# A pre-norm block with routed experts on one core: expert runs in order of size, empty tiles last, four expert tiles between the last token steps

## What is computed

```python
# attn
qkv = einsum('btd,ed->bte', rms_norm(x), w_qkv); q, k, v = split(qkv, 3)
q, k = rms_norm(q), rms_norm(k)
w = exp(k); kv = w * v
y = sigmoid(q) * cumsum(kv, 1) / (cumsum(w, 1) + 1e-6)
u, g = split(einsum('bte,fe->btf', y, w_swiglu), 2)
return x + einsum('btd,ed->bte', u * silu(g), w_out)
# ffn: E = 8 experts, the best K = 2 of each token, summed without weights
logits = flat @ router_weight.T + router_bias
_, topk_idx = top_k(softmax(logits), 2)
y = einsum('th,ehk->tek', flat, weight) + bias[None]
out = take_along_axis(y, topk_idx[:, :, None], axis=1).sum(axis=1)
```

## Time and profile before

| | us |
|---|---|
| median of three runs | 1670.75 (1668.12 to 1671.56) |
| the profiled execution | 1668.43 |
| its span, first to last instruction | 1666.6 |
| TensorE busy | 1589.8 (95%) |
| VectorE busy | 1206.2 (72%) |
| GpSimd busy | 975.3 (59%) |
| ScalarE busy | 568.0 (34%) |
| mean granted TensorE clock | 0.984 of full speed |

### The profile page before, as it was taken

One profiled execution on the slowest core, in us unless ns is written; L12 is line 12 of the kernel. 1 busy time (PEld: TensorE's weight loads), 2 busy tenths in 40 slices (PEclk: granted clock), 3 DMA queues, 4 the chain that ended last, 5 costly groups with the idle time before them and its releaser, 6 DMA issues. The chain is left out here.

```text
span 1666.6 us, 27354 instructions
## 1 busy us (share of the span) xinstructions
PE 1589.8 (95%) x7986; PEld 1298.2 (78%) x7986; DVE 1206.2 (72%) x2434; ACT 568.0 (34%) x1088; POOL 975.3 (59%) x1257
## 2 busy tenths in 40 slices
PE   7999999999999999999999999989999778999987
PEld 4788888788878887887888788778888556888866
DVE  6777778777876787788777767887887465666654
ACT  4333333333333333333333333323332232444432
POOL 4445566575567566755765575557553374666652
PEclk9999999999999999999999999999999897999999
DMA  7022333334333333333333333333424599279996
GB/s 249 29 91 89 115 126 131 119 114 165 115 114 115 115 140 114 137 129 135 133 122 115 115 140 114 115 140 115 140 93 163 151 344 339 84 258 353 383 376 243
DMA packets 138938, 265.64 MB, mean 159 GB/s; under 512 B 18615, under 2 KB 19393, under 8 KB 138794
## 3 DMA queue, kind: packets, MB, share of 16 engines
q1 hardware_dynamic: 121994, 229.70, 39.6%
q0 software_dynamic: 16800, 34.21, 5.9%
HBM read 316.28 MB, written 101.11 MB: 250 GB/s over the span
## 5 line engine op out<-in xcount | busy, mean ns | idle before, releaser
L741 DVE RECIPROCAL B<-B 128x512 f32<-128x512 f32 x64 | 214.6, 3353 | 2.2
L361 POOL TENSOR_SCALAR sa<-ss,hinv,ep 128x1 f32<-128x1 f32 x128 | 44.3, 346 | 211.9 <-ACT B L547 211.2
L446 POOL DMA_INDIRECT out_dram<-B,tab x91 | 94.3, 1036 | 108.9 <-DVE B L817 82.3
L375 POOL TENSOR_TENSOR F<-B,F 128x512 fp32r<-128x512 f32 x64 | 82.4, 1288 | 122.8 <-ACT F L569 122.8
L401 POOL TENSOR_TENSOR B<-B 128x512 f32<-128x512 f32 x112 | 143.3, 1300 | 0.0
L406 POOL TENSOR_TENSOR R<-B,R 128x512 fp32r<-128x512 f32 x112 | 142.0, 1288 | 0.0
L355 POOL TENSOR_SCALAR B<-B,nm,r 128x512 f32<-128x512 f32 x64 | 49.2, 769 | 109.4 <-DVE B L769 109.0
L1238 PE MATMUL pK<-R,F 128*128 128x512 f32 x256 | 108.0, 422 | 1.9 <-DVE B L715 1.9
L1238 PE MATMUL pG<-R,F 128*128 128x512 f32 x256 | 106.8, 417 | 1.9 <-POOL F L375 1.9
L1238 PE MATMUL pU<-R,F 128*128 128x512 f32 x256 | 106.4, 416 | 0.0
L1238 PE MATMUL pV<-R,F 128*128 128x512 f32 x256 | 100.8, 394 | 2.2 <-DVE B L715 2.2
(11 more groups left out here) (237 smaller groups left out, 4606.7 us busy)
## 6 DMA issues: line engine op xcount, KB each, us to landing
R<-pair_weights SPq DMA_DIRECT2D x91, 2048.0 KB
pair_weights<-R SPq DMA_DIRECT2D x112, 512.0 KB, 3.9
B<-in_wm SPq DMA_DIRECT2D x112, 256.0 KB, 3.1
B<-pair_biases SPq DMA_DIRECT2D x91, 256.0 KB
x_scratch<-B SPq DMA_DIRECT2D x64, 264.0 KB, 2.1
B<-in_x SPq DMA_DIRECT2D x64, 256.0 KB, 3.7
B<-in_xt SPq DMA_DIRECT2D x32, 256.0 KB, 3.9
XTB<-in_xt SPq DMA_DIRECT2D x32, 256.0 KB
```

Source lines behind the costliest of these rows:

```text
L361: p.tensor_scalar(sa[:, r, j:j + 1], ss[:, r, j:j + 1], hinv[:, 0:1], ep[:, r:r + 1], ALU.mult, ALU.add).then_inc(s[f"ra{j}"], 1)
L375: p.tensor_tensor(fr(3)[0], DD, fr(2)[1], ALU.subtract).then_inc(s["yl"], 1)
L446: p.indirect_dma_start(od, bass.IndirectOffsetOnAxis(ap=idx[:, J:J + 1], axis=0), YO[J % 3], None, bounds_check=T * 128 - 1, oob_is_err=Fa ...
L741: v.reciprocal(DD, DD).then_inc(s["rec"], 1)
```

## The change

1. `table(0)` orders the early pairs by number of whole tiles, ties by index: a key per pair, a 28x28 comparison, two reductions and a product in place of a running sum. `table(1)` computes each pair's end the same way from the run order.
2. The left-over late runs go to the last pairs of the order and no longer to the first.
3. TensorE's order at the end has four expert runs (0 to 3) between the last token steps, and all engines' orders follow: gathers 0 to 6 are issued in steps 60 to 63, `xn(0)` and `xn(1)` in step 62, `load_pair(3)` ahead of the store of tile Z-1, scatters 0 and 1 ahead of tile Z's normalisation. Runs 1 and 3 keep their transposed parts in slot 2 of R (`HL`), so `load_pair(4)` waits until run 3 is done. `XN[1]` moves to another block of B.
4. In ranks steps two `side` operations at most stand ahead of the gate besides the regular ones, and `side(6)` follows `hc`. In the expert runs `side(9)` takes the place of `side(7)`; the last block's routing starts at J = 6, with RM_J, TT_J, IT_J = 8, 12, 16.

```diff
-        XN = [blk(26), TH_]
+        XN = [blk(26), blk(27)]
...
+        def HL(J):
+
+            if J in (1, 3):
+                at = 2 * 4096 + J // 2 * 1024
+                return R[:, at:at + 512], R[:, at + 512:at + 1024]
+            return fr(2 * (J % 2))[0], fr(2 * (J % 2) + 1)[0]
...
-        RM_J, TT_J, IT_J = 5, 11, 14
+        RM_J, TT_J, IT_J = 8, 12, 16
...
@@ load_pair
+                if t == 4:
+                    e.wait_ge(s["MM"], 4)
...
@@ sync_program
             load_pair(2)
+            load_pair(3)
             store(Z - 1)
-            for t in range(3, 7):
+            for t in range(4, 7):
                 load_pair(t)
...
@@ pool_program
-                if i == Z - 1:
-                    gather(0)
-                    gather(1)
-            for J in range(2, 5):
-                gather(J)
+                if i >= Z - 3:
+                    for J in range(2 * (i - Z + 3), min(2 * (i - Z + 3) + 2, 7)):
+                        gather(J)
             yl(Z)
             x2n(Z - 1)
+            scatter(0)
+            scatter(1)
             x2n(Z)
...
-            asked_ids, asked = False, 5
-            for J in range(1, NJ):
+            asked_ids, asked = False, 7
+            for J in range(3, NJ):
...
@@ table, late
-                    v.tensor_scalar(col, col, -1.0, float(LATE), ALU.mult, ALU.add).then_inc(s["rt"], 1)
...
-                    v.tensor_scalar(c, qnum[:, :], col, None, ALU.is_lt).then_inc(s["rt"], 1)
+                    v.tensor_scalar(col, col, gone, float(NP + 5 - LATE), ALU.add, ALU.add).then_inc(s["rt"], 1)
...
+                    v.tensor_scalar(c, runq[:, :], col, None, ALU.is_gt).then_inc(s["rt"], 1)
...
+                    v.tensor_tensor(before, other(runq[:, :]), of(runq[:, :]), ALU.is_le).then_inc(s["rt"], 1)
...
+                    v.tensor_tensor(before, before, other(f), ALU.mult).then_inc(s["rt"], 1)
...
+                    v.tensor_reduce(end, before, AX.X, ALU.add).then_inc(s["rt"], 1)
...
@@ table, early
-                    v.tensor_tensor_scan(end, ones[:, 0:NP], f, 0.0, ALU.mult, ALU.add).then_inc(s["rt"], 1)
+                    v.scalar_tensor_tensor(out=c, in0=f, scalar=32.0, in1=qnum[:, :],
+                                           op0=ALU.mult, op1=ALU.subtract).then_inc(s["rt"], 1)
...
+                    v.tensor_tensor(before, other(c), of(c), ALU.is_ge).then_inc(s["rt"], 1)
...
+                    v.tensor_reduce(place_, before, AX.X, ALU.add).then_inc(s["rt"], 1)
...
+                    v.tensor_tensor(before, before, other(f), ALU.mult).then_inc(s["rt"], 1)
...
+                    v.tensor_reduce(end, before, AX.X, ALU.add).then_inc(s["rt"], 1)
...
@@ vector_program, token loop
                     if i in RM_I:
                         held[0] = False
-                        side(6)
+                        side(2 if i == RM_I[EB] else 1)
...
                 if i:
                     hc(i - 1)
-                side(m)
+                side(6 if i in RM_I else m)
...
@@ vector_program, runs
+            gl(0)
             scan_kv(Z)
             hl(Z - 1)
-            gl(0)
+            gl(1)
             y_chain(Z)
             x2l(Z - 2)
             lg(Z - 3)
+            gl(2)
             x1(Z - 1)
+            gl(3)
+            xb(0)
+            ya(0)
             gate(Z)
             hc(Z)
             lg(Z - 2)
+            xb(1)
+            ya(1)
             hl(Z)
-            gl(1)
-            xb(0)
-            ya(0)
+            gl(4)
             x2l(Z - 1)
             x1(Z)
...
-                side(7)
+                side(9)
...
@@ tensor_program
                 if i:
                     um(i - 1)
+                if i == Z:
+                    gt(0)
...
             pe_h(Z - 1)
-            gt(0)
+            gt(1)
+            mm(0)
             om(Z - 1)
             pe_r(Z - 2)
             pe_lt(Z - 3)
-            mm(0)
+            gt(2)
+            mm(1)
+            pe_lg(Z - 2)
+            gt(3)
             gm(Z)
-            pe_lg(Z - 2)
             um(Z)
             pe_lt(Z - 2)
+            mm(2)
             pe_h(Z)
-            gt(1)
+            gt(4)
+            mm(3)
             om(Z)
             pe_r(Z - 1)
             pe_lg(Z - 1)
-            for J in range(1, NJ):
+            for J in range(4, NJ):
```

More of the change, by code:

```diff
@@ L642, in scalar_program @@
                     lt(i - 3)
+                if i == Z - 1:
+                    a.wait_ge(s["rt"], tab_done[0])
+                    xn(0)
+                    xn(1)
                 if i == 2:
@@ L645, in scalar_program @@
                     a.activation(wrr[:, :, 0:E], wrs[:, :, :], ACT.Copy).then_inc(s["wrh"], 1)
+            gh(0)
             hh(Z - 1)
-            a.wait_ge(s["rt"], tab_done[0])
-            xn(0)
+            xn(2)
+            gh(1)
             x2t(Z - 2)
-            gh(0)
+            gh(2)
+            xn(3)
             yh(Z)
+            gh(3)
             th(Z)
             lt(Z - 2)
+            xn(4)
             hh(Z)
-            xn(1)
-            gh(1)
+            gh(4)
             x2t(Z - 1)
             lt(Z - 1)
-            xn(2)
+            xn(5)
+            gh(5)
             x2t(Z)
-            gh(2)
-            xn(3)
+            xn(6)
             lt(Z)
-            for J in range(3, NJ):
+            for J in range(6, NJ):
                 if J == EARLY:
@@ L903, in table, with of, other @@
                 o4 = INC[:, 0:6 * NP].bitcast(f32).rearrange("p (a q) -> p a q", a=3)
-                ise, cume = early[:, 2:2 + NP], hold
-                nrun, res, gone = early[:, 0:1], early[:, 1:2], rtmp[:, 231:232]
+                ise, place_ = early[:, 2:2 + NP], hold
+                nrun, gone = early[:, 0:1], early[:, 1:2]
+                before = (B[:, 16 * 512:16 * 512 + NP * NP] if late else XGA[:, 0:NP * NP]).rearrange("p (q o) -> p q o", o=NP)
                 j0, nj = (EARLY, LATE) if late else (0, EARLY)
                 now = slice(j0, j0 + nj)
+                def of(ap):
+                    return ap.unsqueeze(2).broadcast_to([128, NP, NP])
+                def other(ap):
+                    return ap.unsqueeze(1).broadcast_to([128, NP, NP])
                 ready()
@@ L980, in table @@
                     ready()
-                    v.tensor_tensor_scan(cume, ones[:, 0:NP], ise, 0.0, ALU.mult, ALU.add).then_inc(s["rt"], 1)
+                    v.tensor_reduce(nrun, ise, AX.X, ALU.add).then_inc(s["rt"], 1)
                     yield
                     ready()
-                    v.tensor_copy(nrun, cume[:, NP - 1:NP]).then_inc(s["rt"], 1)
-                    yield
-                    ready()
-                    v.tensor_scalar(runq[:, :], cume, 5.0, None, ALU.add).then_inc(s["rt"], 1)
+                    v.tensor_scalar(runq[:, :], place_, 5.0, None, ALU.add).then_inc(s["rt"], 1)
                     yield
@@ L1435, in tensor_program @@
                     ids(1)
-        base = [24 * b for b in range(EB + 1)] + [24 * EB + 25 + 40, 24 * EB + 25 + 40 + 24]
+        base = [24 * b for b in range(EB + 1)] + [24 * EB + 25 + 42, 24 * EB + 25 + 42 + 24]
         marks_made = [n + 20 for n in base]
```

76 lines of the change are left out of this document (38 added, 38 removed).

## The result

The changed kernel takes 1643.09 us, the median of four runs (1642.73 to 1643.74); the kernel before, run beside it, takes 1669.95 (four runs, 1668.12 to 1671.56). The ratio is 0.984, with an interval of 0.9823 to 0.9857: faster by 1.6%. The forecast was 1641, its range 1620 to 1659. The profiled execution took 1643.26 with a span of 1641.2, against a span of 1666.6 before: 25.4 us less.

The account below looks back on a forecast made before the run. TensorE, busy 95% of the span, was taken to bound the kernel. Gains of 5.0 (token loop), 13 (hand-over) and 10.4 (late runs) sum to 28.4 us, giving 1640.0 or 1642.3, called 1641; range 1620 to 1659.

Parts of the forecast that it names:

- A: Whole kernel: the forecast itself, 1641 us, own range 1630 to 1652; chance 0.52.
- Part 1: Ranks steps of the token loop: routing behind the gate cuts TensorE's 1.74 us wait to 0.6; 5.6 us in five steps.
- Part 2: Early table, steps 53 to 55: gate wait shrinks by 3.2 us, a new wait of some 4.1 comes; net -0.9.
- Part 3: Early runs: ordering pairs by size gives 9 loads in place of 12, saving 19 us of DMA in the hand-over.
- Part 4: Last token steps: four runs between them, 26.5 us without a wait; then a 10.4 us wait at run 7's transposes.
- The walk: Last token steps: following the engines' queues with known operation lengths finds no wait, 26.5 us with four runs in it.
- Part 5: Hand-over, nine routing steps a run: runs 6 to 12 take 35.4 us, clock costs 4; gain 13 us.
- Part 6: Runs 20 to 90: empty tiles last relieve late loads; 10.4 us gained, some 2 us of waits near runs 46 to 57.
- B: Hand-over: TensorE sets it, gather 7 lands in time and VectorE keeps pace; 45 us gained, 1624; chance 0.20.
- C: Hand-over gives nothing: clock costs 15 us again, gather 20 comes late; 15.4 us gained, 1654; chance 0.18.
- D: Early runs go one at a time at low clock, 7.9 us each; slower, 1680, deciding from 7.2 us spacing; chance 0.06.
- E: Whole kernel: no effect, hand-over losses eat the gains or the order stays as it was; 1669; chance 0.04.

Follow-up runs that it names:

- run 20: Not a follow-up: the expert run inside the kernel whose start ends the hand-over, at 1400.93 us in the changed kernel's profile.
- run 7: Not a follow-up: an expert run inside the kernel, in the hand-over; TensorE waits 11.44 us before its transposes in the changed kernel.
- run 13: Not a follow-up: an expert run inside the kernel, in the hand-over; the prediction had it start at 84.5 us.
- run 12: Not a follow-up: an expert run inside the kernel, in the hand-over; the prediction gave it 4.4 us.
- run 43: Not a follow-up: an expert run inside the kernel, in the late part; it starts 5.56 us after run 42.
- run 42: Not a follow-up: an expert run inside the kernel, in the late part; TensorE waits 4.45 us before it in the changed kernel's first profile.
- the kernel with rank order: Changed kernel with gathers 7 and 8 issued before four placements, and late pairs also ordered by early size: 1632.30 us, ratio 0.9786 (third chip).
- run 90: Not a follow-up: the last of the kernel's 91 expert runs; from run 20 to it takes 231.6 us in the changed kernel.
- run 0: Not a follow-up: the first of the kernel's 91 expert runs, placed between the last token steps by the change.

## Why the prediction was right, point by point

The forecast was A, and the time came within 2 us of it. Its three terms, 5.0 + 13 + 10.4 = 28.4, were measured as 9.1 + 9.9 + 6.0, and 0.4 behind the last run: 25.4. The errors are +4.1, -3.1, -4.4 and +0.4. That the total came so near is in part luck, since the first cancels more than half of the others, and 1.2 of it is no effect of the change. What holds are the mechanisms and the places that the forecast named, one by one below.

**Part 1: mechanism right, size right.** TensorE's lead over the kernel before grows by 1.74 - 0.53 = 1.21 us at each of five ranks steps, 6.2 in all with what rounding leaves, where I had 5.6, and undoing it gives it back.

**Part 2: the operations right, the net on the wrong side of zero.** VectorE's timeline of the changed kernel in step 53:

```profile
1075.49 1.10 DVE L905 TENSOR_TENSOR CAR<-CAR,INC 128x28 bf16<-128x28 bf16 x1
...
1077.13 0.68 DVE L767 SCALAR_TENSOR_TENSOR B<-B,pG 128x512 f32<-128x512 f32 x1
...
1081.02 0.98 DVE L980 TENSOR_TENSOR XGA<-rtmp 128x784 f32<-128x784 f32 x1
...
1084.42 0.95 DVE L986 TENSOR_TENSOR XGA<-XGA,rtmp 128x784 f32<-128x784 f32 x1
```

A 784-element operation takes 0.95 to 0.98 us, for which I had taken 1.0. The wait at the gate shrinks by 3.28 us, from 4.46 to 1.18 (I had 3.2). The new wait of 4.1 us came as 1.17 + 1.76 + 1.26 in three places, 4.2. But the lead falls by only 2.9 there, and the step nets +0.4, not -0.9. What the sum had left out is the clock behind the wait. Windows of the kernel before behind its 4.46 us, and of the changed kernel behind its 1.18 us:

```profile
1091.00:1094.70 3.70, 3.70 (x12) 2.93 (x11) 3.63 (x8) 0.60 (x1) 0.00 (x0) 0.55 1.04 399
...
1079.90:1083.30 3.40, 3.35 (x16) 2.57 (x16) 3.16 (x7) 0.60 (x1) 0.34 (x1) 1.00 0.49 117
```

Before, the granted clock was 0.55 there and the matmuls of the key projection came 0.43 us apart in place of 0.23; over that projection the lead grows by a further 1.57 us. Another 0.39 is a small wait at 1112.30 in the kernel before.

As a rival I had a price of 1.29 us more, the length of one GpSimd addition, for each of two large operations. The cover that I named held: GpSimd's last addition ended at 1080.24, and the first large operation began at 1081.02 and ran at full pace, while the small L905, at 1075.49, began under a GpSimd addition (from 1075.23) and took 1.10 us, against 0.21 at 1353.49, where GpSimd only issues transfers. The Trainium skill, SBUF — State Buffer, the section "Who interferes with whom", says that a VectorE instruction with two SBUF inputs contends with a GpSimd instruction that reads SBUF. The trace agrees with that for L905 (1.10 us against 0.21); no run here has a large operation beside a GpSimd addition, so the rival price stays untested.

The token loop gave 4.1 us more than the 5.0. Of that 1.2 lies before the fourth step, where nothing is changed and this execution was 1.6 us quicker than most (see the result), so it is no effect of the change (1.6 less 0.4 that it was behind up to there); 0.6 and 1.3 are the sizes above; 1.2 is gained in two places between 1143 and 1185, of which I had no term: 0.55 of it is a wait before the hidden transposes at 1152.18 in the kernel before that the changed kernel does not have, and the rest is not settled; and the last steps gave 0.1 where I had 0.3.

**Part 3: the count right, its effect only partly.** The loads came exactly at runs 0, 3, 6, 9, 11, 13, 15, 17, 19, and the profile moves 258.56 MB in place of 265.64, three loads less. But where I had placed the effect, in the hand-over's DMA, undoing it costs 2.6 to 4.2 us; the 5.9 to 8.5 us behind run 20 I had given no part in it.

**Part 4: right in mechanism and nearly in size.** The walk gave 26.5 us for the last token steps and no wait; measured 26.5. The three waits of some 1.2 us are 1.41, 1.15 and 1.23. The new wait before run 7's transposes is 11.44 (I had 10.4), through gather 7 behind four placements and scatter 2, in flight for 11.6 us where I had taken 9.7. With GpSimd's order changed that wait went and part of it moved to gather 9. The four placements themselves take 5.2 us of GpSimd; gather 7's flight was also shorter then, 7.5 us at most. In the changed kernel SyncE issued weights at 1319.33 and 1324.17, beside gather 7; whether they made its flight longer no run here separates. That four runs between the steps, by themselves, are what fills the 26.5 us was not tried apart: no kernel here undoes that part alone.

**Part 5: the pace right, the clock's term too small, gather 20's landing too long.** From run 6 to run 13 I had 35.4 us and it took 39.1. VectorE's output additions in the changed kernel give the spacings:

```profile
1343.48 0.69 DVE L835 TENSOR_TENSOR B<-pK,B 128x512 f32<-128x512 f32 x1
...
1348.43 0.69 DVE L835 TENSOR_TENSOR B<-pV,B 128x512 f32<-128x512 f32 x1
...
1351.58 0.69 DVE L835 TENSOR_TENSOR B<-pQ,B 128x512 f32<-128x512 f32 x1
...
1357.17 0.69 DVE L835 TENSOR_TENSOR B<-pK,B 128x512 f32<-128x512 f32 x1
...
1364.63 0.69 DVE L835 TENSOR_TENSOR B<-pV,XGA 128x512 f32<-128x512 f32 x1
```

With the two that follow (5.2 and 4.2), the six spacings up to run 12 are 4.95, 3.15, 5.6, 7.5, 5.2 and 4.2, where the sum had 4.9, 3.8, 5.4, 7.1, 4.9 and 4.4 for runs 7 to 12. VectorE's pace was right; TensorE's excess lies at run 6, whose addition came 9.1 us after its first matmul (1334.37), where run 13's came 4.7 after. The clock's term was too small. I took 4 us for it "with fewer, longer waits"; by the same formula, one minus the granted clock, times the window's length, it is 0.18 x 25.3 + 0.15 x 34.6 + 0.12 x 32.9 = 13.7 us, hardly less than the 15 of before. But the formula charges too much: it counts the low clock also for the time in which TensorE stands idle, and in the first of these windows it is busy for 9.7 of 25.3 us. Its busy time in the whole hand-over fell by 7.2 us (99.4 to 92.2), where going from 15 to 4 would have been 11. Against that gather 20 came sooner than I had it: issued at 1390.77, its tile was there 3.4 us later, not 8.5, at a DMA share of 0.70 in that window and not 0.96 (that this is the reason was not tried), and its wait was 1.60 us. So run 20 started 119.3 us after the transposes, not 116.

**Part 6: right at the end, wrong in the middle.** The 20 late loads stand at the runs that the forecast listed, and the last runs wait for nothing. But loads at 41 and 42, in adjacent runs, cost 4.45 us of wait and a low clock right behind it (run 43 follows 5.56 us after run 42, 2.35 more than usual, and the granted clock from 1476.3 to 1485.0 is 0.71), where I had allowed 2 us in all and placed them near runs 46 to 57. This is the term that was mis-sized most, 10.4 for 6.0. Skipping one of the two loads removed all of it. The wait before run 42 differs between profiles of this late order: 1.99 and 4.55 us on the chip of the first experiments, 2.23 and 3.87 on the third.

**The rivals.** B needed gather 7 in time; it came 11 us late. C had the clock near 15 us, as the formula gives it, but TensorE's busy time fell all the same, gather 20 cost a wait of 1.60 us only, and the token loop gave more than in its sum. D needed a mean spacing of 7.2 us: from run 4 to run 20 it was (1400.93 - 1312.83) / 16 = 5.5. Only two spacings of these sixteen exceed 7.2, the 15.8 of the long wait among them. E did not occur.

## What to carry to other kernels

A queue is read by its order: a gather for TensorE's next tile stood behind four issues that nobody waited for (5.2 us), and TensorE waited 11.44 us. Moved ahead, it passed half of the wait on to the next gather that then stood in that place. Where weights stream beside the work, look at the distance between neighbouring loads and not only at their count: two in adjacent runs cost 4.45 + 2.35 us, and on the third chip an order that never puts them nearer than two runs left no wait at all. Distance is not the whole of it: shorter waits also stand before runs 46 and 83, two runs behind the load before. Small side work ahead of a gate that another engine waits for cost its full length in each of five steps (1.1 us of work, 1.21 us of wait). And a low granted clock costs only where the engine works: read its busy time for the same work, not the clock times the window.

## What the runs showed of the hardware that I had not expected

- One wait of 4.46 us in the token loop cost 1.57 us more behind it: the granted clock was 0.55 in the next 3.7 us. Behind the 1.74 us waits of the ranks steps it stayed at 1.00 (470.3 to 474.0). Shortening a wait can so be worth more than its length.
- The granted clock stays at 0.85 and 0.88 for 67 us behind one stretch in which TensorE was busy for 9.7 of 25.3 us, even where its busy share is back at 26.81 of 34.6 and 29.26 of 32.9. What would shorten it no run here shows; in the kernel with rank order, whose longest wait is 6.99 us, 1338 to 1398 still stands at 0.87.
- A row gather's time in flight differs by more than three times: 3.4 us for gather 20, 11.6 us for gather 7, and 11.4 us for gather 9 in the kernel that has 7 first (issue to ScalarE's start).
- The time from the third to the fourth token step comes in two lengths, 18.4 us in three profiles and 19.95 to 20.0 in eleven, for the same instructions. The 1.6 us between them are half of the 0.2% that a measurement of this kernel tells from no change. What decides it no run here shows.
- On the second chip the kernel before was 1.3% slower than on the third (1690.67 to 1668.46) and the changed kernel 1.2% (1659.60 to 1640.45). Of the 18.6 us that the changed kernel's span is longer there than in its first profile, 14.3 lie between run 20 and run 90, where weights are loaded, and 2.0 ahead of run 0.
